# A four-stage transformer-like kernel on one Trainium2 core: slot table begun at half of its one-hots, gather started on source places alone, batch 2's shared products and the layer-2 gating moved

## The chip, the core and the metric

One Trainium2 (trn2) chip, one of its cores. The engines are TensorE (PE, with its weight loads as PEld), VectorE (DVE), ScalarE (ACT), GpSimd (POOL) and SyncE (SP). They run their own instruction streams and wait for one another through semaphores. The metric is the device time of one execution in microseconds; lower is better.

## The reference

Four stages on x of shape (4, 512, 128), each followed by a residual and a layer norm: attention, a mixture of experts (MoE) of 8 experts with one shared expert, a selective scan (state space), and a second, gated MoE with a shared expert. Each token goes to 2 of 8 experts. The two MoE layers are what this case is about; the second one, shortened:

```python
logits = x @ w_router
probs = jax.nn.softmax(logits, axis=-1)
top_w, top_i = jax.lax.top_k(probs, TOP_K)            # TOP_K = 2
mult = top_w / (top_w.sum(axis=-1, keepdims=True) + 1e-08)
w_full = zeros.at[jnp.arange(T)[:, None], top_i].set(mult)
for e in range(num_experts):                          # 8 experts, hidden 512
    h = jax.nn.silu(x @ w_gate[e]) * (x @ w_up[e])
    out = out + w_full[:, e:e + 1] * (h @ w_down[e])
hs = jax.nn.silu(x @ ws_gate) * (x @ ws_up)           # the shared expert
out = out + hs @ ws_down
```

The first MoE has one matrix with silu in place of the gated pair. In the whole, `x = _layernorm(x + stage(x))` four times.

## The kernel before, in words

T = 2048 tokens make 4 batches (b) of 512, or 16 tiles of 128. The layers run one after the other; `l` is 0 for the first MoE and 1 for the second (called layer 1 and layer 2 below). All engines' streams are written out by hand in this order of Python calls; nothing schedules them again.

An MoE layer does not compute all experts for all tokens. The 4096 (token, expert) pairs are sorted by expert into 39 slots of 128 rows (`ROUTED`), and each slot is multiplied with its one expert. To sort, `routing()` on DVE takes the top two experts of each token, PE counts (`counts()`), DVE makes places from the counts, then one-hot matrices: `slot_oh` and `marks` (L1393 to L1396) and the large one, `lane_oh`, 128 x 4096 (L1399). `table()` on PE (L596) multiplies the 32 pair groups' `lane_oh` with `marks`, 32 matmuls into PSUM bank 1; the sums hold for each slot row which token it gets. DVE meanwhile works out which expert each slot has (`past`, `slot_ef`, `slot_e`, L1402 to L1405, semaphore `expert_set`), then reads the table (L1411 to L1415: `source`, the token of each slot row; L1416 and L1417: `dest`, where the result row goes).

POOL then gathers the rows of the 39 slots from HBM with indirect DMAs (`rows<-xn_rows,source`, L1801), eight ahead into a ring, and scatters the slots' results (`y_choice`, L1807) by `dest`. Its first gather waits for `idx_set`, which the last of these DVE instructions raises.

The slot loop (`slot_steps`) is a software pipeline: PE turns the gathered rows of slot i+2 (L635 in layer 2, L663 in layer 1), DVE copies them to `xT` (L1441), PE multiplies slot i+1 (L641 and L645 in layer 2; L668 in layer 1), then slot i's down product. In layer 2 the gate and up weights of the slot's expert are first copied to fixed places: `own_g` by ACT, `own_u` by DVE (`own_weights`, L1434). After the loop, `combine` on DVE adds the two choices of each token, weighted with `gates`, which `gating()` (L1424 to L1430) has made.

The shared expert is done by batch: `shared_up`, then `shared_down` (L511, PSUM bank `2 + b % 2`), then `add_base` on DVE (L1479) adds x and frees the bank. `base_set` counts the `add_base`s. Batch 2 of layer 2 could reuse bank 2 only once batch 0's `add_base` had read it. In layer 2 the order on PE was `shared_down` of batches 0 and 1, the table, `shared_down` of batch 2; then PE waits for `base_set` to reach 3 before the slot loop. On DVE it was `lane_oh` (which waits for batch 1's `shared_down`, since it overlays that one's input), the slot experts, `add_base` 0 and 1, the table's reading, `add_base` 2, gating, `own_weights` of slots 0 and 1, the slot loop. In layer 1 the two `add_base`s and gating already stood behind the table's reading.

Of the kernel before, what the change touches and what calls it, by code (L numbers as in the profile page):

```python
# [20 lines left out]
ALU = mybir.AluOpType  # L21
# [4 lines left out]
P = 128  # L26
# [62 lines left out]
def build(nc, a, out):  # L89
    ctx = ExitStack()  # L90
    with ctx:
# [186 lines left out]
        onehot_set = layers("onehot_set", 1); table_ps = layers("table_ps", 1)  # L278
        expert_set = layers("expert_set", 1); idx_set = layers("idx_set", 1)
# [41 lines left out]
        x_bank, y_bank = ((0, 6), (0, 3)), ((1, 7), (1, 2))  # L321
        def slot_steps(step):

            for i in range(-2, ROUTED + 1):
                step(i)
# [110 lines left out]
        def _(pe):  # L436
# [68 lines left out]
            def shared_down(l, b, parts=range(QT)):  # L505
                pe.wait_ge(*sT_set[l].at((b + 1) * HB))
                if b >= 2:
                    pe.wait_ge(*base_set[l].at(b - 1))
                for q in parts:
                    for j in range(HB):  # L510
                        last = mm_(ps[:, 2 + b % 2, q * P:(q + 1) * P], (own_T[b] if l else sT[b % 2])[:, j, q * P:(q + 1) * P],  # L511
                                   (wd if l else w2)[:, NE * HID + j * D:NE * HID + (j + 1) * D], start=(j == 0), stop=(j == HB - 1))
                if QT - 1 in parts:
                    last.then_inc(sy_ps[l].sem, 1)
# [61 lines left out]
            def moe(l):  # L576
# [15 lines left out]
                def table():  # L592

                    pe.wait_ge(*onehot_set[l].at(1))
                    for g in range(PAIRS):
                        last = mm_(ps[:, 1, 0:2 * ROUTED], lane_oh[:, g, :], marks[:, g, :, :].rearrange("p c s -> p (c s)"),  # L596
                                   start=(g == 0), stop=(g == PAIRS - 1))
                    last.then_inc(table_ps[l].sem, 1)
# [6 lines left out]
                if l == 0:  # L605
                    shared_up(l, 1, (3,))
                    shared_down(l, 0)
                    shared_up(l, 2)
                    shared_down(l, 1)
                    table()  # L610
                    shared_up(l, 3)
                else:
                    shared_down(l, 0)
                    shared_down(l, 1)
                    table()
                    shared_down(l, 2)
# [622 lines left out]
        def _(dve):  # L1239
# [110 lines left out]
            def moe(l):  # L1350
# [8 lines left out]
                def routing():  # L1359
# [37 lines left out]
                    if l:  # L1397
                        dve.wait_ge(*sy_ps[1].at(2))
                    V.tensor_tensor(lane_oh, lane[:, :].unsqueeze(2).to_broadcast(by_lane),  # L1399
                                    count_up[:, :].unsqueeze(1).to_broadcast(by_lane), ALU.is_equal).then_inc(onehot_set[l].sem, 1)  # L1400
# [6 lines left out]
                    if l:  # L1407
                        add_base(l, 0)
                        add_base(l, 1)
# [5 lines left out]
                    link(V.tensor_scalar(source[:, :], held_i[:, :], T - 1, None, ALU.bitwise_and))  # L1415
# [35 lines left out]
                if l == 0:  # L1451
                    add_base(l, 0)
                    add_base(l, 1)
                else:
                    add_base(l, 2)
                gating()

                if l:
                    dve.wait_ge(*expert_set[1].at(1))
                    dve.wait_ge(*sT_set[1].at(3 * HB))  # L1460
                    own_weights(0)
                    own_weights(1)
                slot_steps(step)


                if l:
                    for b in range(NB):
# [8 lines left out]
            def add_base(l, b):  # L1476
                dve.wait_ge(*sy_ps[l].at(b + 1))
                dve.wait_ge(*(normed_set if l else kept)[l].at(b + 1))
                V.tensor_tensor(tiles(base[l][:, b * S:(b + 1) * S]), x_seq(b), tiles(bank(2 + b % 2)),  # L1479
# [199 lines left out]
        def _(pool):  # L1679
# [110 lines left out]
            def moe(l):  # L1790
# [6 lines left out]
                for i in range(ROUTED + RING):  # L1797
# [6 lines left out]
                    if i >= RING:  # L1804
                        y = i - RING
                        pool.wait_ge(*yout_set[l].at(y + 1))
# [57 lines left out]
```

## Time and profile before

| what | value |
|---|---|
| median of 3 runs | 665.77 us (664.08 to 669.92) |
| profiled execution | 664.27 us, its span 662.5 us |
| granted TensorE clock, mean | 0.95 |
| PE busy | 548.3 us (83%) |
| DVE busy | 420.4 us (63%) |
| POOL busy | 383.3 us (58%) |
| ACT busy | 361.1 us (55%) |

Layer 1's MoE lies at about 70 to 205 us of the span, the state space at 205 to 485, layer 2's MoE from 485 to the end. The granted clock is in shares of the full 2.4 GHz: 0.50 is 1.2 GHz. The profile gives for each instruction its start and length, the idle time of its engine before it in brackets, and what ended that idle time.

### The profile page before, as it was taken

What the parts mean: (1) busy time and instruction counts of PE and PEld (TensorE: products, weight loads), DVE (VectorE), ACT (ScalarE), POOL (GpSimd) and SP (SyncE); (2) the same over time, 40 slices, a digit from 0 to 9 for tenths busy, and PEclk for the clock granted to TensorE, in tenths of its full rate; (3) what the DMA queues carried; (4) which work ended last, traced back from release to release, by engine and by line L of the source; (5) the groups of instructions that cost most, each with busy time, mean ns of one, the idle gap of its engine ahead of it and who ended that gap; (6) DMA issues with size and microseconds to landing.
All of it is one profiled execution on the core that took longest, in us unless ns stands there. A gap on an engine that the chain in (4) does not pass through costs nothing.

```text
span 662.5 us, 8697 instructions
## 1 busy us (share of the span) xinstructions
PE 548.3 (83%) x2858; PEld 368.3 (56%) x2858; DVE 420.4 (63%) x754; ACT 361.1 (55%) x640; POOL 383.3 (58%) x303
## 2 busy tenths in 40 slices
PE   6988889999997559769967986989686899999980
PEld 3666556777665224225323532433246799999950
DVE  3444581111106899999999999999969444444446
ACT  3544564665552657944895597768332155555423
POOL 1011117777771246996697689678830677677451
PEclk9999998999999879889988998899998899999986
DMA  4154102111117754344334434433200111111142
GB/s 111 50 176 151 42 4 52 46 50 52 45 40 234 326 190 146 139 147 142 129 141 165 127 127 146 160 124 130 81 16 1 40 42 48 43 43 45 28 130 63
DMA packets 35147, 65.78 MB, mean 99 GB/s; under 512 B 6111, under 2 KB 23207, under 8 KB 34464
## 3 DMA queue, kind: packets, MB, share of 16 engines
q1 hardware_dynamic: 29824, 51.19, 22.9%
q0 software_dynamic: 4992, 9.32, 5.4%
q10 hardware_dynamic: 288, 4.72, 2.0%
q8 instruction: 24, 0.39, 0.2%
q14 instruction: 19, 0.16, 0.1%
HBM read 57.60 MB, written 8.52 MB: 100 GB/s over the span
## 4 chain that ended last, share of the span: by engine, by line
PE 39%; DVE 32%; issue 10%; POOL 8%; ACT 6%; DMA 5%; SPq 0%; DVEq 0%; POOLq 0%; ACTq 0%
DVE wide L1625 11%; DVE ps L1618 6%; PE ps L641 5%; PE ps L645 5%; DVE w L1625 5%; PE ps L653 5%; PE ps L668 4%; PE ps L681 4%; PE ps L792 3%; ACT work L1163 2%; PE ps L674 2%; DVE work L1490 2%; DVE work L1399 1%; POOL y_choice L1807 1%; POOL wide L1773 1%
## 5 line engine op out<-in xcount | busy, mean ns | idle before, releaser
L1801 POOL DMA_INDIRECT rows<-xn_rows,source x78 | 76.0, 974 | 61.5 <-DVE dest L1417 38.3
L1625 DVE TENSOR_TENSOR_SCAN wide<-work,ps 128x1024 f32<-128x1024 f32 x43 | 98.2, 2284 | 1.3
L792 PE MATMUL ps<-wide,ident 128*128 128x512 f32 x128 | 70.0, 675 | 26.7 <-POOL wide L1773 26.7
L1618 DVE TENSOR_TENSOR ps<-ps,w 128x1024 f32<-128x1024 f32 x64 | 78.9, 1233 | 7.1 <-DVE w L1625 0.5
L1441 DVE COPY xT<-ps 128x128 f32<-128x128 f32 x78 | 22.3, 287 | 81.7 <-PE ps L663 81.7
L1773 POOL TENSOR_TENSOR wide<-wide,w 128x1024 f32<-128x1024 f32 x22 | 51.8, 2356 | 32.9 <-DVE wide L1625 31.7
L792 PE MATMUL ps<-w,ident 128*128 128x512 f32 x124 | 61.4, 623 | 10.7 <-POOL w L1773 10.7
L1163 ACT ACTIVATE work<-work,a_neg 128x512 f32<-128x512 f32 x86 | 56.7, 711 | 19.8 <-DVE wide L1625 17.4
L1446 DVE TENSOR_TENSOR wide<-wide,ps 128x512 f32<-128x512 f32 x39 | 26.8, 687 | 61.9 <-PE ps L645 60.7
L792 PEld LDWEIGHTS ps<-wide,ident 128*128 128x128 f32 x128 | 24.1, 201 | 62.1 <-POOL wide L1773 39.9
L1773 POOL TENSOR_TENSOR w<-wide,w 128x1024 f32<-128x1024 f32 (+1 forms) x21 | 48.9, 2331 | 12.5 <-DVE wide L1625 12.2
L1807 POOL DMA_INDIRECT y_choice<-yout,dest x40 | 41.5, 1038 | 22.9 <-issue 11.4
L792 PEld LDWEIGHTS ps<-w,ident 128*128 128x128 f32 x124 | 24.8, 205 | 46.8 <-issue 25.3
L1807 POOL DMA_INDIRECT y_choice<-pre,dest x38 | 39.7, 1046 | 19.1 <-issue 9.4
L1625 DVE TENSOR_TENSOR_SCAN w<-rows,ps 128x1024 f32<-128x1024 f32 x21 | 48.0, 2284 | 0.6
L641 PE MATMUL ps<-xT,wide 128*128 128x128 f32 x312 | 42.1, 279 | 2.3 <-DVE xT L1441 2.3
L668 PE MATMUL ps<-w,xT 128*128 x78 | 41.9, 620 | 0.9 <-DVE xT L1441 0.9
L1026 ACT ACTIVATE wide<-ps 128x512 f32<-128x512 f32 x39 | 23.3, 597 | 35.4 <-PE ps L668 35.4
L645 PE MATMUL ps<-xT,wide 128*128 128x128 f32 x312 | 42.1, 279 | 0.0
L653 PE MATMUL ps<-wd,wide 128*128 x312 | 41.3, 275 | 0.0
L681 PE MATMUL ps<-w,wide 128*128 x312 | 41.2, 275 | 0.0
L641 PEld LDWEIGHTS ps<-xT,wide 128*128 128x128 f32 x312 | 38.7, 195 | 2.5 <-DVE xT L1441 2.5
(273 smaller groups left out, 1172.9 us busy)
## 6 DMA issues: line engine op xcount, KB each, us to landing
w<-bc_rows SPq DMA_DIRECT2D x64, 512.0 KB, 3.7
w<-in_w ACTq DMA_DIRECT2D x2, 2304.0 KB, 9.1
w<-y_choice SPq DMA_DIRECT2D x16, 256.0 KB, 3.8
wg<-in_wg SPq DMA_DIRECT2D x1, 2304.0 KB, 12.1
wu<-in_wu SPq DMA_DIRECT2D x1, 2304.0 KB, 17.0
wd<-in_wd SPq DMA_DIRECT2D x1, 2304.0 KB, 22.0
rows<-xn_rows,source POOLq DMA_INDIRECT x78, 2.5
work<-in_x SPq DMA_DIRECT2D x4, 256.0 KB, 2.9
```

What stands on the lines that cost most here:

```text
L641: last = mm_(ps[:, hbank[0] + p, j * P:(j + 1) * P], own_g[p][:, j * P:(j + 1) * P], xT[p][:, :], start=True, stop=True)
L645: last = mm_(ps[:, hbank[1] + p, j * P:(j + 1) * P], own_u[p][:, j * P:(j + 1) * P], xT[p][:, :], start=True, stop=True)
L653: last = mm_(bank(y_bank[1][p], D), hs[p][:, j * P:(j + 1) * P], wc[:, ds(e + j * D, D)], start=(j == 0), stop=(j == HB - 1))
L668: last = mm_(bank(hbank[0] + p), xT[p][:, :], wa[:, ds(e, HID)], start=True, stop=True)
L681: last = mm_(bank(y_bank[l][p], D), hT[p][:, j * P:(j + 1) * P], wc[:, ds(e + j * D, D)], start=(j == 0), stop=(j == HB - 1))
L792: last = mm_(bank(6 + h), ident[:, :], hc[j % 4][:, h, :], start=False, stop=(j == NS - 1))
L1163: last = A(dA[n % 3][:, h, lo:S], delta[n // NS % 2][:, h, lo:S], ACT.Exp, scale=a_neg[:, j + h * NS:j + h * NS + 1])
L1618: V.tensor_tensor(dbu, du, bc_all[j % 4][:, 0:S].unsqueeze(1).to_broadcast([P, EH, S]), ALU.mult)\
L1625: V.tensor_tensor_scan(st[n % 3].rearrange("p h t -> p (h t)"), dA[n % 3].rearrange("p h t -> p (h t)"), dbu.rearrange("p h t -> p (h t)") ...
L1773: G.tensor_tensor(hc[j % 4][:, 0:own, :], st[n % 3][:, 0:own, :], bc_all[j % 4][:, S:2 * S].unsqueeze(1).to_broadcast([P, own, S]), ALU.mu ...
L1801: G.indirect_dma_start(out=xin[i % RING][:, :], out_offset=None, in_=xn_rows, in_offset=bass.IndirectOffsetOnAxis(ap=source[:, i:i + 1], a ...
L1807: G.indirect_dma_start(out=y_choice, out_offset=bass.IndirectOffsetOnAxis(ap=dest[:, y:y + 1], axis=0), in_=yout[y % RING][:, :], in_offse ...
```

## The change

Five edits:

1. `lane_oh` is made in two DVE instructions of 128 x 2048 in place of one of 128 x 4096, each raising `onehot_set`. `table()` waits for the first ahead of matmul 0 and for the second ahead of matmul 16. Both layers.
2. `idx_set` is raised twice: by the instruction that makes `source`, and by the one that makes `dest`. The gather waits for the first; the first scatter waits for the second. Both layers.
3. Layer 2, PE: `shared_down` of batch 2 stands ahead of the table. It writes bank 7 (`sy_bank`) in place of bank 2, and no longer waits for batch 0's `add_base`.
4. Layer 2, DVE: `add_base` 0 and 1 stand behind the table's reading, with `add_base` 2.
5. Layer 2, DVE: `gating()` stands behind the slot loop, ahead of `combine`.

The diff, cut to these:

```diff
-        onehot_set = layers("onehot_set", 1); table_ps = layers("table_ps", 1)
-        expert_set = layers("expert_set", 1); idx_set = layers("idx_set", 1)
+        onehot_set = layers("onehot_set", 2); table_ps = layers("table_ps", 1)
+        expert_set = layers("expert_set", 1); idx_set = layers("idx_set", 2)
...
+        def sy_bank(l, b):
+
+            return 7 if l and b == 2 else 2 + b % 2
...
             def shared_down(l, b, parts=range(QT)):
                 pe.wait_ge(*sT_set[l].at((b + 1) * HB))
-                if b >= 2:
+                if b >= 2 and not (l and b == 2):
                     pe.wait_ge(*base_set[l].at(b - 1))
                 for q in parts:
                     for j in range(HB):
-                        last = mm_(ps[:, 2 + b % 2, q * P:(q + 1) * P], (own_T[b] if l else sT[b % 2])[:, j, q * P:(q + 1) * P],
+                        last = mm_(ps[:, sy_bank(l, b), q * P:(q + 1) * P], (own_T[b] if l else sT[b % 2])[:, j, q * P:(q + 1) * P],
...
                 def table():
 
-                    pe.wait_ge(*onehot_set[l].at(1))
                     for g in range(PAIRS):
+                        if g % (PAIRS // 2) == 0:
+                            pe.wait_ge(*onehot_set[l].at(g // (PAIRS // 2) + 1))
...
                     shared_down(l, 0)
                     shared_down(l, 1)
+                    shared_down(l, 2)
                     table()
-                    shared_down(l, 2)
...
-                    V.tensor_tensor(lane_oh, lane[:, :].unsqueeze(2).to_broadcast(by_lane),
-                                    count_up[:, :].unsqueeze(1).to_broadcast(by_lane), ALU.is_equal).then_inc(onehot_set[l].sem, 1)
+                    by_half = [P, PAIRS // 2, P]
+                    for i in range(2):
+                        own = slice(i * PAIRS // 2, (i + 1) * PAIRS // 2)
+                        V.tensor_tensor(lane_oh[:, own, :], lane[:, own].unsqueeze(2).to_broadcast(by_half),
+                                        count_up[:, :].unsqueeze(1).to_broadcast(by_half), ALU.is_equal).then_inc(onehot_set[l].sem, 1)
...
-                    if l:
-                        add_base(l, 0)
-                        add_base(l, 1)
                     dve.wait_ge(*table_ps[l].at(1))
...
-                    link(V.tensor_scalar(source[:, :], held_i[:, :], T - 1, None, ALU.bitwise_and))
+                    V.tensor_scalar(source[:, :], held_i[:, :], T - 1, None, ALU.bitwise_and).then_inc(idx_set[l].sem, 1)
...
                 else:
-                    add_base(l, 2)
-                gating()
-
-                if l:
                     dve.wait_ge(*expert_set[1].at(1))
                     dve.wait_ge(*sT_set[1].at(3 * HB))
+                    for b in range(3):
+                        add_base(l, b)
                     own_weights(0)
                     own_weights(1)
+                if l == 0:
+                    gating()
                 slot_steps(step)
 
                 if l:
+                    gating()
                     for b in range(NB):
...
+                        if y == 0:
+                            pool.wait_ge(*idx_set[l].at(2))
                         pool.wait_ge(*yout_set[l].at(y + 1))
```

What this does to the order of the instructions, at three places of layer 2. First PE, from the counts to the first slot: L589 and L590 are the counts, L511 `shared_down`, L596 the table, L635 the turned rows of slots 0 and 1, L641 slot 0's gate product. Before:

```order
L589 MATMUL ps<-mask,before 128x128
L590 MATMUL ps<-mask,ones 128x128
L511 MATMUL ps<-wd,work 128x128 x32
L596 MATMUL ps<-work 128x78 x32
L511 MATMUL ps<-wd,work 128x128 x16
L635 MATMUL ps<-ident,rows 128x128 x2
L641 MATMUL ps<-xT0,wide 128x128 x4
```

And now (the lines have moved by 4 and 5):

```order
L593 MATMUL ps<-mask,before 128x128
L594 MATMUL ps<-mask,ones 128x128
L515 MATMUL ps<-wd,work 128x128 x48
L601 MATMUL ps<-work 128x78 x32
L640 MATMUL ps<-ident,rows 128x128 x2
L646 MATMUL ps<-xT0,wide 128x128 x4
```

The 16 products of batch 2 have moved from behind the table to ahead of it. Second DVE, from `lane_oh` to the first reading of the table. Before:

```order
L1399 TENSOR_TENSOR work<-lane,count_up 128x4096
L1402 TENSOR_TENSOR work<-slot_row,ends 128x312
L1404 TENSOR_REDUCE slot_ef<-work 128x39
L1405 TENSOR_SCALAR slot_e<-slot_ef 128x39
L1479 TENSOR_TENSOR work<-x_all,ps 128x512 x2
L1411 COPY vacant<-ps 128x39
```

And now:

```order
L1407 TENSOR_TENSOR work<-lane,count_up 128x2048 x2
L1410 TENSOR_TENSOR work<-slot_row,ends 128x312
L1412 TENSOR_REDUCE slot_ef<-work 128x39
L1413 TENSOR_SCALAR slot_e<-slot_ef 128x39
L1416 COPY vacant<-ps 128x39
```

The one-hots are in two pieces, and the two `add_base`s (L1479) are gone from ahead of the reading. Third DVE, from `dest` to the first weight copies. Before:

```order
L1417 SCALAR_TENSOR_TENSOR dest<-held,vacant 128x39
L1479 TENSOR_TENSOR work<-x_all,ps 128x512
L1424 TENSOR_REDUCE zsum<-sc 128x16
L1425 TENSOR_SCALAR zsum<-zsum 128x16
L1426 TENSOR_TENSOR den<-zsum,egap 128x16
L1429 RECIPROCAL gates0<-den 128x16
L1430 TENSOR_TENSOR gates1<-gates0,egap 128x16
L350 TENSOR_LOAD slot_e
L1434 ISA
L1434 COPY wide<-wu 128x512
L1434 ISA
L1434 COPY wide<-wu 128x512
```

And now:

```order
L1422 SCALAR_TENSOR_TENSOR dest<-held,vacant 128x39
L1485 TENSOR_TENSOR work<-x_all,ps 128x512 x3
L354 TENSOR_LOAD slot_e
L1439 ISA
L1439 COPY wide<-wu 128x512
L1439 ISA
L1439 COPY wide<-wu 128x512
```

Behind `dest` there are now three `add_base`s and no gating. In layer 1 only the one-hots are in two pieces; its DVE and PE order is otherwise the same.

## Rows read from the trace of the kernel before

**Rows 1.** Chain that ended last, 485 to 530 us: start, length (us), engine, tile, line

```profile
505.72 4.34 DVE work L1399
510.11 2.26 PE ps L596 x32
512.37 4.67 PE ps L511 x32
520.73 1.67 PE ps L641 x8
```

**Rows 2.** Timeline, layer 1, table: start, length, engine, line, tiles, [idle before <-releaser]

```profile
88.36 4.42 DVE L1399 TENSOR_TENSOR work<-lane,count_up 128x4096 bf16<-128x4096 bf16 x1
...
92.83 1.35 PE L596 MATMUL ps<-work 128*128 128x78 bf16 x32 [1.05 <-DVE work L1399]
...
93.71 0.18 DVE L1405 TENSOR_SCALAR slot_e<-slot_ef 128x39 int32<-128x39 f32 x1
...
94.22 0.20 DVE L1411 COPY vacant<-ps 128x39 f32<-128x39 f32 x1 [0.33 <-PE ps L596]
...
95.45 0.20 DVE L1417 SCALAR_TENSOR_TENSOR dest<-held,vacant 128x39 uint32<-128x39 f32 x1
```

**Rows 3.** Timeline, layer 1, gathers and scatters on POOL, slot 1's turn on PE

```profile
96.59 1.23 POOL L1801 DMA_INDIRECT rows<-xn_rows,source  x1 [22.88 <-DVE dest L1417]
...
98.13 0.94 POOL L1801 DMA_INDIRECT rows<-xn_rows,source  x1 [0.30 <-issue]
...
100.70 0.33 PE L663 MATMUL ps<-ident,rows 128*128 128x128 f32 x1 [0.88 <-DMA rows<-xn_rows,source]
...
109.02 1.03 POOL L1807 DMA_INDIRECT y_choice<-yout,dest  x1 [1.22 <-ACT yout L912]
...
195.64 0.98 POOL L1807 DMA_INDIRECT y_choice<-pre,dest  x1 [1.17 <-ACT pre L912]
```

**Rows 4.** Timeline, layer 2, from shared_down to dest

```profile
496.49 7.31 PE L511 MATMUL ps<-wd,work 128*128 128x128 f32 x64
...
511.09 1.28 DVE L1479 TENSOR_TENSOR work<-x_all,ps 128x512 f32<-128x512 f32 x2
...
512.41 0.20 DVE L1411 COPY vacant<-ps 128x39 f32<-128x39 f32 x1
...
513.20 0.18 DVE L1415 TENSOR_SCALAR source<-held_i 128x39 uint32<-128x39 uint32 x1
...
513.64 0.20 DVE L1417 SCALAR_TENSOR_TENSOR dest<-held,vacant 128x39 uint32<-128x39 f32 x1
```

**Rows 5.** Timeline, layer 2, from the first gather to the first xT copies

```profile
514.12 1.11 POOL L1801 DMA_INDIRECT rows<-xn_rows,source  x1 [15.45 <-DVE dest L1417]
515.54 0.95 POOL L1801 DMA_INDIRECT rows<-xn_rows,source  x1 [0.30 <-issue]
...
517.07 0.69 DVE L1479 TENSOR_TENSOR work<-x_all,ps 128x512 f32<-128x512 f32 x1 [3.23 <-PE ps L511]
...
519.64 0.84 DVE L1434 COPY wide<-wu 128x512 f32 x2 [0.77 <-DVE gates L1430]
520.40 0.47 DVE L1441 COPY xT<-ps 128x128 f32<-128x128 f32 x2
```

**Rows 6.** Busy by stretch, layer 2: length; PE, PEld, DVE, ACT, POOL (instructions); clock, DMA, GB/s

```profile
510.10:512.20 2.10, 2.09 (x33) 2.09 (x33) 2.03 (x5) 0.37 (x1) 0.00 (x0) 0.50 0.00 0
512.20:517.10 4.90, 4.83 (x35) 4.64 (x32) 1.45 (x9) 0.78 (x2) 2.36 (x3) 0.78 0.06 13
...
520.70:524.10 3.40, 3.37 (x17) 3.37 (x18) 0.17 (x1) 1.11 (x2) 2.67 (x3) 0.57 0.29 60
524.10:527.00 2.90, 2.90 (x26) 2.90 (x25) 2.04 (x4) 0.60 (x1) 0.95 (x1) 0.91 0.20 51
```

**Rows 7.** The slot loop of layer 2 by stretch, columns as in rows 6

```profile
528.30:614.80 86.50, 86.50 (x778) 86.50 (x777) 38.10 (x93) 43.55 (x94) 63.32 (x61) 1.00 0.17 43
```

**Rows 8.** Timeline, layer 2, DVE's first combine

```profile
638.98 3.32 DVE L1490 SCALAR_TENSOR_TENSOR work<-w,gates,work 128x128 f32<-128x128 f32 x8 [8.79 <-DMA w<-y_choice]
```

More of the change, by code:

```diff
@@ L1478, in add_base @@
                 dve.wait_ge(*(normed_set if l else kept)[l].at(b + 1))
-                V.tensor_tensor(tiles(base[l][:, b * S:(b + 1) * S]), x_seq(b), tiles(bank(2 + b % 2)),
+                V.tensor_tensor(tiles(base[l][:, b * S:(b + 1) * S]), x_seq(b), tiles(bank(sy_bank(l, b))),
                                 ALU.add).then_inc(base_set[l].sem, 1)
```

## The prediction

> **What bounds the kernel now.** I read the chain that ended last first, for the two places that the change touches, then the timelines there, then the busy shares by stretch to see who paces what follows. The reader is to see three things.
>
> In layer 2 the chain from the routing to the first slot is DVE's `lane_oh` (505.72 to 510.06), PE's table (to 512.37), PE's `shared_down` of batch 2 (to 517.04), and, after DVE's `add_base` 2, gating and weight copies, slot 0's first product at 520.73 [rows 1, 5]. Of these only the table is needed for the slots' rows. PE finished batches 0 and 1 at 496.49 + 7.31 = 503.80 [rows 4] and then stood idle until 510.11, because the table waited for the one-hots.
>
> From there on the slot loop belongs to PE: in 528.30 to 614.80 it is busy 86.50 of 86.50 us at a granted clock of 1.00 [rows 7]. A slot has 25 PE records (1 turn and three times 8), so 778 records are 31.1 slots of 2.78 us. Nothing in the loop has slack for PE, and nothing else holds it, so the loop's end moves with its start.
>
> In layer 1 POOL paces. From its first scatter at 109.02 it goes on with 0.30 us between instructions until one waits for ACT at 195.64 [rows 3]; 31 gathers and 36 scatters of about 1.0 us with those gaps fill that time. So here too an earlier first gather, and with it an earlier first scatter, moves the layer's end.
>
> **The change, layer 1.** The one-hots ended at 88.36 + 4.42 = 92.78, the table ran 92.83 to 94.18, and DVE, done with the slot experts at 93.71 + 0.18 = 93.89, waited 0.33 us for it [rows 2]. Two halves cost the fixed part of one more DVE instruction: not under nothing, not over 0.18 us, which is what a whole 128x39 instruction takes [rows 4]. Neighbours that don't depend on each other overlap a little, so I take 0.1. PE does the first 16 matmuls during the second half, and the last 16 take half of 1.35, 0.68, from 92.93 to 93.6. That is ahead of DVE's slot experts (93.99 with the 0.1), so DVE goes on without a wait at about 93.95 instead of 94.22, 0.27 earlier. `source` is done 0.97 us after that start (in layer 2, 512.41 to 513.38 [rows 4]), at 94.92. The gather waited for `dest`, done at 95.65 [rows 2]. The release comes 0.73 earlier. The gather started 0.94 after its release (96.59 [rows 3]), against 0.28 in layer 2 (513.84 to 514.12 [rows 4, 5]); no row says what the other 0.66 is. If it goes with the release it stays, and the gain is 0.73; if it was a fixed moment that the first gather had to wait for, the gain is between 0.07 and 0.73; if it vanishes, 1.39. I take **0.7**, since the rows show nothing that POOL waits for but `dest`. The table's earlier end also starts `shared_up` of batch 3 about 0.6 earlier, which keeps ACT's last silu out of the way. The scatter's new wait for `dest` is met 13 us before the first scatter and costs nothing; even if the cover were gone it would be 0.46, the distance from `source` to `dest`.
>
> **Layer 2, the table.** Batch 2's 32 matmul records now run from 503.80 and take half of 7.31, 3.66, at the full clock at which the 64 before them ran: to 507.5. They need no bank wait, and their input was ready (PE never stopped for it before). The first half of the one-hots is there at 505.72 + 2.2 = 507.95, so they are hidden with 0.45 us to spare. The second half is there at 510.16; its 16 matmuls take 0.68 at full clock and 1.13 at the lower one (half of 2.26 [rows 1], a stretch at 0.50 [rows 6]); PE has just worked, so I take 0.7 and the table is done at 510.9. DVE's slot experts end at 511.2 (the `add_base` behind them started at 511.09 [rows 4], plus 0.1). So DVE reads the table at **511.2, not 512.41**: the table and the two `add_base`s that ended together at 512.37 are both off the path. `source` is done at 512.17, the first gather starts 0.28 later at 512.45 instead of 514.12 [rows 5], 1.67 earlier.
>
> **Layer 2, the first slot.** Two chains meet. DVE: `dest` at 512.63, three `add_base`s of 1.28 + 0.69 = 1.97 [rows 4, 5], so 514.60; then the 0.77 us of reading `slot_e` into registers that stood ahead of the weight copies [rows 5], so these start at 515.37; `xT` follows 0.76 after (519.64 to 520.40 [rows 5]), at 516.13, and the first one is done at about 516.4. Gathers: the second one starts 1.42 after the first, at 513.87; in layer 1 PE turned the same slot 2.57 after that gather's start (98.13 to 100.70 [rows 3]), so 516.44. PE does slot 1's turn ahead of slot 0's product, so that begins about 0.25 later, at **516.7 instead of 520.73, 4.0 earlier**. The two chains are within 0.3 us, so one of them being off doesn't cost much, one of them being late costs all that it is late.
>
> What I cost at nothing: gating, 1.1 us (five small instructions between the end of `add_base` 2 at 517.76 and the register load at 519.64 - 0.77 = 518.87 [rows 5]), now behind the loop, where DVE waited 8.79 us for the scattered rows [rows 8]; without that cover 1.1 us. The three `add_base`s ahead of the weight copies hold back PE too (it waits for `base_set` at 3), but that is 514.60, ahead of the first turn. ACT's `own_g` copies wait for `slot_e`, 0.1 later than before and with some 4 us in hand.
>
> **The clock.** It was 0.50 in the table's stretch after 6.3 us of idle PE, 0.78 in the next one, 0.57 at the first slot and 0.91 after it [rows 6]. In full-clock time the first slots lost 3.40 x 0.43 + 2.90 x 0.09 = 1.72 us. With the change PE is idle from 510.9 to 516.7 but for two turns, 5.8 us where it was 3.7, so the start may look like the table's: 2.10 x 0.50 + 4.90 x 0.22 = 2.13 lost. The difference, **0.4**, is a cost of the change; it is between nothing (the same loss as before) and the rival below. The Trainium skill, "TensorE: Matmul & The Clock Gate", Part 1, says the idle state of the array is the throttled one and activity releases it, and that idle gaps cost a new warm-up; rows 6 show the 0.50 after the idle stretch and the return during work. By that page's rule the longer idle ahead of the loop speaks against the change, and what the rule would make of it at worst is the third rival.
>
> **Sum.** 0.7 + 4.0 - 0.4 = 4.3 us. Against the profiled execution's own 664.27: 660.0. The median of the runs is 665.77, 1.5 above it, with 664.08 the lowest, so the same sum against the median is 661.5. I take 660.8, between.
>
> **Rivals.**
> - *A late landing or a stall at the first slots takes back 1 to 2 us* (20%). For it: everything up to the first slot is a chain of small links, each of which showed spread (0.28 and 0.94 from release to first gather [rows 3 to 5]); a second gather that lands 1 us late moves slot 0 by 1 us, and so does a slower register load. Against: nothing in rows 5 stalled. Gain 2.3 to 3.3: 661 to 662 on the profile's time, up to 663.5 on the median's.
> - *More than the sum* (10%): layer 1's 0.66 vanishes and the clock costs nothing more, 0.66 + 0.4 on top: gain 5.4, 658.9 to 660.4.
> - *Slower: the clock stays low into the loop* (5%). The idle stretch ahead of the loop is longer, and the first slots have waits on silu and on DVE between products, so PE might not come back after two slots. Each slot done at half clock costs 2.78 us more [rows 7]. The gain of 4.3 is gone after 1.5 such slots beyond those of before, and 1% is lost after 4 (4 x 2.78 = 11.1, so 671 on the profile's time). Against: in rows 6 the clock came back to 0.91 within the second slot though its waits were the same.
> - *The change does not reach the loop* (5%): if slot 0 were held by something that doesn't move, as ACT's weight copies, only the 0.7 of layer 1 and what of the gather's 1.67 counts would stay: 662 to 663.6.
>
> **How the numbers follow.** The forecast itself, a gain of 3.3 to 5.2, has 60%: 659.1 to 662.5 between both bases. The range leaves out the clock's bad case and the far end of each of the others: 657.5 to 664.5. About 1% (6.7 us) is what a measurement of this kernel can tell from no change; the runs of before lie 5.8 apart. A gain over 6.7 needs the second rival and a low draw: 8%. A loss over 6.7 needs four slots at half clock: 3%. Within 1%: 89%.
>
> **What would show it.** Right: the table's second half 16 matmuls right behind the second half one-hots, DVE going on from `slot_e` to reading the table without idle in both layers; the first gather of layer 2 about 1.7 us earlier in distance from `lane_oh`'s start (6.7 instead of 8.4), slot 0's product at 11.0 from it instead of 15.0; gating right behind the loop with DVE still idle ahead of `combine`; slots of 2.79 us. Wrong: a clock of 0.50 over more than the first two slots; idle time of PE ahead of slot 0 longer than to 11 us from `lane_oh`'s start, and then what releases it (the gather, DVE's `xT`, ACT); in layer 1 a first gather less than 0.5 us earlier, or POOL idle between scatters.

## Result and the profile after

| | before | after |
|---|---|---|
| median of 20 runs each on one chip | 669.49 us (663.89 to 671.97) | 664.65 us (660.34 to 667.02) |
| ratio, 95% interval | | 0.9937 (0.9918 to 0.9956) |
| profiled execution: time, span | 664.27, 662.5 us | 663.71, 661.9 us |
| mean granted clock | 0.95 | 0.94 |
| PE, DVE, POOL, ACT busy | 548.3, 420.4, 383.3, 361.1 us | 554.6, 419.7, 383.4, 361.4 us |

The change gains 0.63% of 669.49, 4.2 us (4.8 by the two medians), where 4.3 was forecast. That is inside the 1% which the prediction took as no change, though the interval of 20 and 20 executions leaves out 1. The time itself, 664.65, lies 0.15 above the range, because the forecast started from too low a base. The 20 times of before fall into two groups with nothing between 665.8 and 668.4: five from 663.89 to 665.77 and fifteen from 668.49 to 671.97. The profile shown of before (664.27) is of the lower group, and so are two of the three runs shown. Those of after: two at 660.34 and 660.87, eighteen from 663.50 to 667.02, the profiled one (663.71) among these. Lower group against lower group (medians) it is 664.65 to 660.6, upper against upper 669.70 to 664.8. So the two profiles differ by 0.56 us only, while the kernels differ by 4.2.

The timeline of after in layer 2, from the one-hots to the first slots, in the columns of [rows 2]. The one-hots begin at 508.40, against 505.64 before (in the DVE timeline; the chain of [rows 1] has 505.72); distances below are from that start.

```profile
508.40 4.48 DVE L1407 TENSOR_TENSOR work<-lane,count_up 128x2048 bf16<-128x2048 bf16 x2
...
510.74 0.76 PE L601 MATMUL ps<-work 128*128 128x78 bf16 x16 [0.60 <-DVE work L1407]
512.94 0.76 PE L601 MATMUL ps<-work 128*128 128x78 bf16 x16 [1.44 <-DVE work L1407]
513.92 0.19 DVE L1416 COPY vacant<-ps 128x39 f32<-128x39 f32 x1
515.17 1.11 POOL L1807 DMA_INDIRECT rows<-xn_rows,source  x1 [13.73 <-DVE source L1420]
515.19 1.88 DVE L1485 TENSOR_TENSOR work<-x_all,ps 128x512 f32<-128x512 f32 x3
516.99 0.80 DVE L1439 COPY wide<-wu 128x512 f32 x2
517.98 0.45 PE L640 MATMUL ps<-ident,rows 128*128 128x128 f32 x1 [4.27 <-DMA rows<-xn_rows,source]
519.15 0.48 PE L640 MATMUL ps<-ident,rows 128*128 128x128 f32 x1 [0.73 <-DMA rows<-xn_rows,source]
519.42 1.92 PE L646 MATMUL ps<-xT,wide 128*128 128x128 f32 x8
521.13 1.91 PE L650 MATMUL ps<-xT,wide 128*128 128x128 f32 x8
```

It is what the change was to do: half of the table's matmuls run during the second half of the one-hots, the other half (0.76 us) behind it, the gather is released by `source`, three `add_base`s stand behind `dest`, and slot 0's product starts at 519.42 - 508.40 = 11.02 from the one-hots' start, where before had 520.73 - 505.64 = 15.09. Slot 0's two groups of eight products take 1.92 and 1.91 us, at half clock. The chain of waits of after for the same place (start, length, what):

```profile
508.48 4.40 DVE work L1407 x2
512.88 0.41 DVE work L1410
...
513.32 0.49 DVE slot_ef L1412
...
514.70 0.20 DVE source L1420
514.90 0.28 issue
515.17 1.11 POOL rows L1807
516.28 0.30 issue
516.59 2.52 DMA rows<-xn_rows,source
519.11 0.04 issue
519.15 0.48 PE ps L640
```

Against [rows 1], PE's table and `shared_down` are gone from it; DVE's slot experts and the landing of the second gather stand in their place.

### The profile page after: what moved, and what is told of

The parts are those of the page before. It is cut to its first block, busy times and chain, and to the rows that moved or that the text cites. A ratio compares the mean times of both kernels' runs of the same rounds, so it can differ in the third digit from the quotient of the medians.

```text
span 661.9 us, 8700 instructions
## 1 busy us (share of the span) xinstructions
PE 554.6 (84%) x2858; PEld 370.4 (56%) x2858; DVE 419.7 (63%) x756; ACT 361.4 (55%) x640; POOL 383.4 (58%) x303
## 4 chain that ended last, share of the span: by engine, by line
PE 36%; DVE 34%; issue 10%; POOL 9%; ACT 6%; DMA 3%; SPq 0%; POOLq 0%; DVEq 0%; ACTq 0%
DVE wide L1631 11%; DVE ps L1624 6%; PE ps L646 5%; PE ps L650 5%; DVE w L1631 5%; PE ps L658 5%; PE ps L673 4%; PE ps L797 3%; PE ps L686 3%; ACT work L1168 2%; PE ps L679 2%; POOL rows L1807 2%; DVE work L1496 2%; POOL y_choice L1815 1%; DVE work L1407 1%
## 5 line engine op out<-in xcount | busy, mean ns | idle before, releaser
L797 PE MATMUL ps<-wide,ident 128*128 128x512 f32 x128 | 72.1, 691 | 24.6 <-POOL wide L1779 24.6
L797 PE MATMUL ps<-w,ident 128*128 128x512 f32 x124 | 63.5, 641 | 10.5 <-POOL w L1779 10.5
```

What stands on the lines that cost most here:

```text
L797: last = mm_(bank(6 + h), ident[:, :], hc[j % 4][:, h, :], start=False, stop=(j == NS - 1))
```

## What holds the last norm: where the two groups come from

The traces differ ahead of the part that was changed. Before layer 2's one-hots, PE waits 1.94 us for the last layer norm in both kernels. The PE timeline of before:

```profile
490.64 0.66 PE L809 MATMUL ps<-ident,x_all 128*128 128x128 f32 x4 [1.94 <-ACT x_all L1139]
...
491.64 1.03 PE L819 MATMUL ps<-gate,nT_all 128*128 128x8 f32 x8 [0.35 <-ACT nT_all L912]
...
492.53 1.10 PE L501 MATMUL ps<-nT_all,wg 128*128 128x512 f32 x2
```

and of after:

```profile
490.41 1.00 PE L814 MATMUL ps<-ident,x_all 128*128 128x128 f32 x4 [1.94 <-ACT x_all L1144]
...
491.55 1.84 PE L824 MATMUL ps<-gate,nT_all 128*128 128x8 f32 x8
493.24 2.06 PE L505 MATMUL ps<-nT_all,wg 128*128 128x512 f32 x2
```

The same instructions behind the same wait take 0.66, 1.03 and 1.10 us in the one and 1.00, 1.84 and 2.06 in the other. The busy shares by stretch (columns as in [rows 6]) give the clock, first of before:

```profile
490.40:494.00 3.60, 3.01 (x16) 2.09 (x17) 1.12 (x6) 0.85 (x3) 0.79 (x1) 1.00 0.24 73
```

then of after:

```profile
490.50:494.00 3.50, 3.36 (x13) 2.71 (x14) 0.51 (x3) 0.77 (x2) 0.47 (x1) 0.51 0.25 75
494.00:497.00 3.00, 3.00 (x5) 1.22 (x4) 2.25 (x13) 0.00 (x0) 0.00 (x0) 0.50 0.00 0
```

It was 1.00 before and about 0.50 (1.2 of 2.4 GHz) after, from the wait until 497. From ACT's last piece of the norm (489.71 before, 489.48 after) to the one-hots that is 505.64 - 489.71 = 15.93 us against 508.40 - 489.48 = 18.92, 3.0 us. I take this distance, **norm to one-hots**, from every run below. (The expectations of after again and w_before count it from DVE's part of the norm, 1.0 to 1.3 us earlier.)

So the 0.56 us between the two profiles can be added up: 0.23 earlier at the last norm, 2.99 later from there to the one-hots, 3.28 earlier from these to slot 0's result: 0.52. With the clock at the norm taken out, the two profiles differ by 0.56 + 2.99 = 3.55 us.

## Experiments

The runs came from four chips. On that of m1 to m4 (one edit taken back each) before took 669.08 us; on the other three 703 to 705. Ratios are always against before on the same chip. "First result" is ACT's first copy of a slot's result (`yout`).

**Before again, and PE kept busy at the two waits.** The first experiments fill PE's waits with products of 128x512 that nobody reads. `fill(2)` stands ahead of the last norm in w_last, `fill(4)` ahead of layer 2's slots in w_slots; w_all has both, and one such product ahead of layer 1's slots.

```diff
+            def fill(n):
+                for _ in range(n):
+                    mm_(bank(0), ident[:, :], nT_all[:, 0:S], start=True, stop=True)
...
             shared_up(1, 2, (0, 1))
+            pe.wait_ge(*nT_set[1].at(NB - 1))
+            fill(2)
             turn_last()
...
-                pe.wait_ge(*expert_set[l].at(1))
                 pe.wait_ge(*counts_taken[l].at(1))
+                if l:
+                    fill(4)
+                pe.wait_ge(*expert_set[l].at(1))
                 pe.wait_ge(*base_set[l].at(2 + l))
```

> The kernel before, unchanged, profiled once more. Theory 'clock lottery': its times lie in two groups (about 664 to 666 and 668.5 to 672), and they differ in whether TensorE's granted clock falls in PE's wait for the last layer norm, ahead of layer 2's last router products. In a run of the slow group the stretch of 485 to 500 us shows 0.50 during those products (none in the profile shown) and the one-hots of layer 2 start 3 us or more later than at 505.6; in a run of the fast group both are as in the profile shown. Rival 'memory': the slow group's extra time lies in the state space or in the weight loads (205 to 485 us), and the stretch 485 to 500 is the same in both.

> The changed kernel with two more 128x512 products, whose result nobody reads, in PE's wait for the last layer norm (layer 2, ahead of the last turn). They take 1.7 of about 2.1 us that PE is idle. Clock lottery: the granted clock stays 1.00 from 485 to 500 us in every profile, and the median comes down by 2 to 3 us against the changed kernel (ratio to before 0.989 to 0.991 in place of 0.9937), with few runs left in the slow group. Rival: the slow group has its time elsewhere, the median stays within 1 us of the changed kernel's (ratio about 0.9937).

> The changed kernel with four such products (3.4 us) in PE's wait between the table and the first gathered rows of layer 2. If the 0.50 at the first slots is a cost of the idle stretch, the clock stays 1.00, and the distance from the one-hots' start to the loop's steady beat shrinks by 1.7 to 2.3 us; slot 0's product still starts 11.0 us after the one-hots' start. Rival: the first slots are held by the chain of silu, product and weight copies and not by the clock, and the distance shrinks by less than 0.5.

> The changed kernel with both fillings and one such product in layer 1 between shared_up of batch 3 and the first gathered rows. If the clock costs add up, 4 to 6 us below the changed kernel's median: ratio to before 0.984 to 0.988. In layer 1 one product fills 0.86 of 3.5 us, so there the 0.50 may stay. Rival: no more than w_last or w_slots alone.

Measured, before 703.92: before again 0.9994 (0.9972 to 1.0016), w_last 0.9897 (0.9867 to 0.9927), w_slots 0.9945 (0.9920 to 0.9971), w_all 0.9893 (0.9858 to 0.9927). The timeline of w_last (its first row counts the filling too):

```profile
511.29 1.88 PE L453 MATMUL ps<-nT_all,ident 128*128 128x512 f32 x4
...
513.38 0.66 PE L819 MATMUL ps<-ident,x_all 128*128 128x128 f32 x4 [0.22 <-ACT x_all L1151]
...
514.39 1.03 PE L829 MATMUL ps<-gate,nT_all 128*128 128x8 f32 x8 [0.35 <-ACT nT_all L924]
```

The wait is 0.22 instead of 1.94, the products behind it take 0.66 and 1.03 as in the lower group's profile, norm to one-hots is 15.92. Before again, with the unfilled wait, had 19.06. w_all was forecast at 0.984 to 0.988 if the clock's costs added up; it came out at that of w_last, so its rival held. The filling ahead of the slots did its work there and no more. The timeline of w_slots:

```profile
538.40 1.07 PE L653 MATMUL ps<-xT,wide 128*128 128x128 f32 x8
...
543.10 1.06 PE L653 MATMUL ps<-xT,wide 128*128 128x128 f32 x8
...
545.63 0.61 PE L657 MATMUL ps<-xT,wide 128*128 128x128 f32 x4 [0.92 <-issue]
548.03 2.07 PE L665 MATMUL ps<-wd,wide 128*128 x8 [1.78 <-DVE wide L1458]
```

Slot 0's product runs at full clock (1.07), and slot 2's begins 543.10 - 527.55 = 15.55 from the one-hots' start, 2.7 ahead of after (526.63 - 508.40 = 18.23). Yet behind slot 2's start PE stands 0.92 us waiting on issue and 1.78 us for DVE, its next products take 2.07 us, half clock again, and the first result comes 19.67 us from the one-hots' start, where after again has 19.66. The time, 0.9945, is that of the change without the filling (0.9941 below). In the seven profiled executions of after again, w_last, w_slots, w_all, c_w_last, c_w_all and m5, all on these three chips, the first result lies at 19.62 to 19.76, though slot 0's product starts at 10.85 to 11.63: on them it is not slot 0's product that sets it. What does was not found. The slot loop has such stalls throughout there (last section); a chip of the 665 us kind wasn't tried with it, so whether the first slots' clock is worth anything there stays open.

**One edit taken back at a time**, the other four kept. The edits by the numbers of the change: m1 makes the one-hots in one instruction (1), m2 lets the gather wait for `dest` (2),

```diff
-                pool.wait_ge(*idx_set[l].at(1))
+                pool.wait_ge(*idx_set[l].at(2))
```

m3 puts batch 2's `shared_down` behind the table, still in bank 7 (3), and m4 the `add_base`s 0 and 1 ahead of its reading (4):

```diff
-                    shared_down(l, 2)
                     table()
+                    shared_down(l, 2)
...
+                    if l:
+                        add_base(l, 0)
+                        add_base(l, 1)
                     dve.wait_ge(*table_ps[l].at(1))
```

> The changed kernel with edit 1 taken back (one DVE instruction of 128x4096 for the one-hots). All numbers in us from the start of layer 2's one-hots; the changed kernel has table read at 5.52, gather at 6.77, slot 0's product at 11.02. By the prediction's steps the table starts at 4.5 and takes 1.35 at full clock, so DVE waits for it until 5.87: gather at 7.1, product at 11.35; with the clock at half, table read at 6.8, gather 8.0, product 12.3. If the halves bring nothing (DVE's slot experts are the end anyway) nothing moves.

> The changed kernel with edit 2 taken back (the gather waits for dest as before). Us from the start of layer 2's one-hots: gather at 7.1 in place of 6.77, product at 11.35 in place of 11.02, because slot 0's product follows the second gather's landing; in layer 1 the gather 0.3 later (7.75 in place of 7.43). Rival: DVE's three add_bases and weight copies are what slot 0 waits for, and the product stays at 11.0.

> The changed kernel with edit 3 taken back in its order (batch 2's shared_down behind the table, still in bank 7). Us from the start of layer 2's one-hots: gather unchanged at 6.77; shared_down ends at 9.0 at full clock or up to 10.3 at half, add_base 2, the weight copies and xT behind it, slot 0's product at 11.5 to 12.8. Rival: the gathers are the later chain anyway and the product stays at 11.0.

> The changed kernel with edit 4 taken back (add_base of batches 0 and 1 ahead of the reading of the table). Us from the start of layer 2's one-hots: table read at 6.8 in place of 5.52, gather at 8.05, slot 0's product at 12.3 in place of 11.02, as the second gather's landing decides. If the DVE chain decided, the product would stay, since DVE's sum is the same.

| distance from the one-hots' start, layer 2, us | before | after | m1 | m2 | m3 | m4 |
|---|---|---|---|---|---|---|
| table read by DVE | 6.77 | 5.52 | 5.86 | 5.53 | 5.80 | 6.71 |
| first gather | 8.48 | 6.77 | 7.12 | 7.10 | 7.06 | 7.97 |
| slot 0's product | 15.09 | 11.02 | 11.38 | 11.31 | 13.67 | 12.29 |
| first result | 21.60 | 18.32 | 18.65 | 18.47 | 18.55 | 19.13 |
| fifth result | 32.75 | 29.48 | 29.81 | 29.62 | 29.70 | 30.29 |
| ratio to before | 1 | 0.9937 | 0.9916 | 0.9958 | 0.9945 | 0.9978 |
| its 95% interval | | .9918-.9956 | .9879-.9953 | .9919-.9997 | .9918-.9973 | .9949-1.0007 |

m1, m2 and m4 came out within 0.1 us of what was expected of the distances. The times can't tell m1, m2 and m3 from the whole change, nor from each other; m4, the edit that is worth most alone, lies highest, though its interval overlaps theirs. Taken back singly, the four cost 0.33, 0.14, 0.22 and 0.81 us at the fifth result, 1.5 together of the 3.27 that all five bring (the fifth was taken back on another chip): each opens only as far as the others let it.

m3 was a miss. Its gather was expected unchanged at 6.77 and came at 7.06, since the table's halves took 1.22 us each, half clock, in place of 0.76. Slot 0's product was expected between 11.5 and 12.8 and came at 13.67. Its timeline:

```profile
517.63 6.12 PE L515 MATMUL ps<-wd,work 128*128 128x128 f32 x32
...
525.74 1.16 PE L646 MATMUL ps<-xT,wide 128*128 128x128 f32 x8 [0.65 <-DVE xT L1446]
526.73 1.06 PE L650 MATMUL ps<-xT,wide 128*128 128x128 f32 x8
```

PE had stood 4.17 us ahead of the table and 0.98 within it; the granted clock is 0.50 over the table and 0.61 over the 32 products behind it, which take 6.12 us in place of 3.6. So `add_base` 2 and all behind it are late. But PE then meets the slots at full clock (1.16, 1.06 against 1.92, 1.91), and the first result is 0.23 later only. The order of after pays for its earlier start with a slow clock in the slots; the other order runs the same slow stretch off before them.

**The change again, gating taken back, and before with the filling**, on a chip where before took 703.23. m5 has `gating()` back behind the three `add_base`s (5); w_before is the kernel before with `fill(2)` ahead of the last norm.

> The changed kernel once more, against the kernel before on the same chip. If the change is worth its 4.3 us whatever the clock does at the last norm, the ratio is 0.992 to 0.995 again. From the start of layer 2's one-hots: gather 6.77, slot 0's product 11.0 again; from the last norm's application to the one-hots either 16.9 or 20.2, the two states of the clock.

> The changed kernel with edit 5 taken back (gating between the add_bases and the weight copies). Us from the start of layer 2's one-hots: DVE ends the add_bases at 8.7, gating at 9.8, the copies at 10.6 (11.4 if the 0.77 of register load comes back), xT at 10.9 to 11.7. The second gather's row is turned by 11.0. So slot 0's product moves by 0 to 0.7 in place of the whole 1.1. By the recorded prediction, whose two chains were within 0.3, it moves by about 0.8.

> The kernel before with the two unread products in PE's wait for the last norm, and nothing else. Clock lottery: the distance from the last norm's application to the one-hots is 16.9 to 17.2 in place of 20.3, and the median is 2.5 to 3.3 us under the kernel before's (ratio 0.995 to 0.996). It has none of the five edits, so what it gains is the clock's alone. Rival: no difference.

After again 0.9941 (0.9918 to 0.9965): the same gain on the other kind of chip. m5 0.9960 (0.9934 to 0.9987): slot 0's product at 11.63, 0.6 later than in after again, within the 0 to 0.7 expected. From the timeline of m5:

```profile
537.41 0.76 DVE L1439 COPY wide<-wu 128x512 f32 x2 [0.77 <-DVE gates L1435]
...
538.43 2.07 PE L646 MATMUL ps<-xT,wide 128*128 128x128 f32 x8 [0.40 <-DVE xT L1446]
```

Now PE waits for DVE. But the first result stands at 19.65 against 19.66 in after again, so on this chip nothing of the 0.6 was left there; edit 5 alone is not shown to be worth anything. w_before 0.9962 (0.9943 to 0.9981), 2.7 us of 703.23, with none of the five edits; norm to one-hots 15.92. m5, without filling, had 15.92 too and was profiled at 697.03, the lowest of its ten.

**The filling once more, and useful work in its place**, before 704.92. In u_useful the table stands ahead of batch 2's `shared_down` and `add_base` 2 behind the weight copies, so that PE works right up to the slots without reading dummies; u_both adds the last norm's `fill(2)`.

```diff
-                    shared_down(l, 2)
                     table()
+                    shared_down(l, 2)
...
-                    for b in range(3):
-                        add_base(l, b)
+                    add_base(l, 0)
+                    add_base(l, 1)
                     own_weights(0)
                     own_weights(1)
+                    add_base(l, 2)
```

> The changed kernel with two unread products in PE's wait for the last norm, again, beside three others on one chip. Ratio to the kernel before 0.989 to 0.991: the change's 4.3 us and the 3 us of the clock in three executions of four.

> The changed kernel with unread products in all three waits (two at the last norm, four between layer 2's table and its gathered rows, one in layer 1). Where no engine stalls on instruction issue in the slot loop, the 2.3 us that the filling of the second wait brings from the one-hots to slot 1's product reach the end: first result copied 16.0 us after the one-hots' start in place of 18.3, and the ratio is 0.986 to 0.988. If the loop takes it back, the ratio is that of the run with the last norm's filling alone.

> The changed kernel with batch 2's shared_down behind the table again, as useful work in the wait for the gathers, and DVE's order add_base 0 and 1, weight copies, add_base 2. Us from the start of layer 2's one-hots: shared_down ends at 9.0 to 11.7 by the clock that it finds, slot 0's product at 11.0 to 13.2 but at full clock, first result copied at 16.2 to 18.0 in place of 18.32. Ratio 0.991 to 0.994. Rival: it ends like the run with edit 3 alone taken back, first result at 18.55 and no gain.

> The kernel of u_useful with two unread products in PE's wait for the last norm. 3 us under u_useful in three executions of four: ratio 0.987 to 0.990.

Measured: c_w_last 0.9921 (0.9890 to 0.9952), c_w_all 0.9920 (0.9893 to 0.9948), u_useful 0.9979 (0.9954 to 1.0003), u_both 0.9933 (0.9910 to 0.9956). c_w_all has its first result at 19.76, where 16.0 was expected if the loop did not take it back: its other case held, the ratio is that of c_w_last. u_useful was expected at 0.991 to 0.994, with the first result at 16.2 to 18.0. It failed for m3's reason, as its timeline shows:

```profile
535.63 5.87 PE L515 MATMUL ps<-wd,work 128*128 128x128 f32 x32
...
543.12 1.16 PE L646 MATMUL ps<-xT,wide 128*128 128x128 f32 x8 [0.28 <-DVE xT L1446]
```

The products run at half clock for most of their 5.87 us (granted 0.63); slot 0's begin at 13.05 and the first result comes at 20.54, 0.9 behind after again. u_both, with its median 3.1 us under that of u_useful, gains it back at the last norm, but misses its 0.987 to 0.990. The changed kernel with `fill(2)` at the last norm has 0.9897 and 0.9921 of before (0.9893 and 0.9920 with the other fillings too), the changed kernel alone 0.9937 and 0.9941. So it is the best version by its point values. It was never timed beside the changed kernel on one chip, and its intervals overlap that one's (0.9918 to 0.9956), so how much better it is than the change alone is not shown; the filling's own worth is measured on the kernel before (w_before).

Over all profiled executions, norm to one-hots was 15.92 or 15.93 us in six of six with that filling, and without it 15.92 or 15.93 in two of eleven (before and m5) and 18.92 to 19.29 in nine (before again, after, after again, m1 to m4, w_slots, u_useful). In six of these nine the four turns right behind the wait still took 0.65 or 0.66 us, full clock, and only the products behind them 1.44 to 1.85. So the same program comes out of this one wait either way (before 15.93, before again 19.06, on different chips), and PE's idle time decides it, since filling it removes the slow case. That it is drawn anew in each execution is inferred from the times of one chip, which fall into groups.

The mean granted clock, which every execution has, goes with the groups on the chips of 665 to 670 us. Of after's 20 it is 0.950 in the two lowest and at most 0.949 in the others. Of the 27 executions of before on the chip of m1 to m4, the nine from 663.84 to 667.01 have 0.950, the eighteen from 667.61 to 673.10 have 0.938 to 0.948. On that chip the gap between the groups is not empty, though (666.04, 667.01, 667.61), and one execution of m4 has 0.950 at 666.56. That the last norm makes the whole of the groups is not shown: they lie 4 to 5 us apart, the distance explains 3.0 to 3.4. And executions differ ahead of it too: on these chips the last norm (ACT's last piece) is reached at 489.71 (before), 489.48 (after), 493.94, 488.46, 492.78 and 489.70 (m1 to m4), and m1 and m3, the latest, were the longest of their eight executions. What moved them was not looked into.

## Why the prediction was right or wrong

**The base: the failed step.** "I take 660.8, between" took the profile's 664.27 and the median of three, 665.77. Both are of the lower group, one execution in four of this kernel; the sum of 4.3 from 669.49 gives 665.2, 0.5 from the measured 664.65. The sign was in front of me: one of the three runs, 669.92, stood 5.8 above the lowest, and I named that spread only as a bound on what can be measured, where it should have widened the range upward. What the runs show in its place is a base of 669.49, with fifteen of twenty executions at 668.49 or above; 3.0 of the 5 us between the groups go with the clock at the last norm, and the rest stays open. The changed kernel's own lower group lies at 660.6, near the 660.0 predicted from the lower group's profile, but it is two runs in twenty.

**Layer 1: 0.7, measured 0.77 to 0.80.** Timeline of after, layer 1:

```profile
93.01 0.76 PE L601 MATMUL ps<-work 128*128 128x78 bf16 x16 [0.54 <-DVE work L1407]
...
93.98 0.19 DVE L1416 COPY vacant<-ps 128x39 f32<-128x39 f32 x1
...
95.07 0.20 DVE L1422 SCALAR_TENSOR_TENSOR dest<-held,vacant 128x39 uint32<-128x39 f32 x1
95.89 1.23 POOL L1807 DMA_INDIRECT rows<-xn_rows,source  x1 [22.08 <-DVE dest L1422]
```

DVE reads the table at 93.98 without a wait (forecast 93.95), `source` ends at 94.94 and the gather starts 0.95 later: the 0.94 of [rows 3] went with its release, as taken; what it is stays unknown. The row puts the gather's wait down to `dest`, which ended at 95.27, though the code waits for `source` alone, and m2 shows the difference: with the wait for `dest` it starts 0.32 later. From the one-hots' start the gather moved from 8.23 to 7.43 and the first scatter from 20.66 to 19.89. Of that 0.77, 0.54 was left at the scatter that waits for ACT (195.64 [rows 3], now 195.10), since these one-hots began 0.10 later and the loop took 0.13 longer; 0.46 at layer 1's `combine` and 0.23 at the last norm. These last steps are the difference of one execution of each and may be noise: m1 to m4 reach the last norm up to 5.5 us apart. The prediction let all of layer 1's 0.7 reach the end; no run shows that it did.

**Slot 0's product: 4.0, measured 4.07.** Forecast 11.0 from the one-hots' start, measured 11.02. The gather chain gave it, link by link: table read at 5.52 (forecast 5.5), gather at 6.77 (6.7), the turn of slot 1 at 10.75 (10.7). The DVE chain, which I put within 0.3 us of it, was 1.1 faster than forecast: the weight copies started at 516.99, 8.6 us from the one-hots' start where the sum has 9.7, before the last `add_base` had ended in the record, and the 0.77 us of reading `slot_e` ahead of them [rows 5] did not appear. In m5, with gating there again, it did. So the read follows gating's last small instruction at a price and the `add_base`s at none; why, no run here shows.

**The clock: 0.4, measured 0.8, the one term that was mis-sized.** From slot 0's product to the first result it took 21.60 - 15.09 = 6.51 us before and 18.32 - 11.02 = 7.30 after. Busy by stretch of after:

```profile
516.40:520.40 4.00, 1.69 (x7) 1.43 (x8) 1.97 (x6) 0.00 (x0) 2.90 (x4) 0.50 0.20 49
520.40:524.40 4.00, 4.00 (x21) 4.00 (x20) 1.22 (x3) 1.11 (x2) 3.08 (x4) 0.50 0.28 51
524.40:528.40 4.00, 4.00 (x36) 4.00 (x36) 1.23 (x3) 1.99 (x4) 2.12 (x3) 0.96 0.22 53
```

The start did not look like the table's stretch, as assumed. PE ran at 0.50 from slot 0's product at 519.42 to 524.7: about 5.3 x 0.50 = 2.65 us lost where before had lost 1.72 and I had put 2.13. It had been idle for 4.27 us ahead of the first turn. m3 and w_slots are the counterproof: with work there, slot 0's two products run at full clock (1.16 and 1.06 us in the one, 1.07 and 1.06 in the other). The gain at the first result is therefore 4.07 - 0.79 = 3.28 and not 3.6, and with layer 1's 0.77, if all of it reached the end, the sum is 4.05. The two profiles, with the clock at the norm taken out, have 3.55, which is 3.28 and the 0.23 of layer 1 that was left. Measured are 4.2 by the ratio (2.9 to 5.5 by its interval), and 4.05 and 4.9 from group to group. So the mechanism was right, but that 4.3 meets 4.2 this closely is in part luck: the interval would have held 3.5 as well. The Trainium skill, "TensorE: Matmul & The Clock Gate", Part 1, says that one and the same kernel has more or fewer slow matmuls from run to run, by the phase at its start, and that the ramp costs less than 1% of a typical kernel. The traces agree in size (3.0 us of 664), but show the draw at a wait in the middle of the kernel, and it was larger than all errors of the sum together.

**The loop and gating.** The loop's row of after, against [rows 7]:

```profile
528.90:615.20 86.30, 86.30 (x776) 86.30 (x775) 37.95 (x94) 43.55 (x93) 63.01 (x61) 1.00 0.17 45
```

PE is busy throughout again, so its start sets its end: the last gate product stands at 626.93, from 627.45. Gating lies behind the loop and is hidden, as the DVE timeline shows:

```profile
629.59 0.28 DVE L1429 TENSOR_REDUCE zsum<-sc 128x16 f32<-128x128 f32 x1
...
638.37 3.33 DVE L1496 SCALAR_TENSOR_TENSOR work<-w,gates,work 128x128 f32<-128x128 f32 x8 [7.58 <-DMA w<-y_choice]
```

DVE's wait for the rows fell from 8.79 [rows 8] to 7.58, the 1.2 us of gating.

**The rivals.** A late landing (20%) did not come: each link named above was on time. More than the sum (10%): neither of its conditions held. The slow clock into the loop (5%) did not come: it was back at 524.7, within slot 1. The change not reaching the loop (5%): it reached it whole. What decided the number had no rival: that the kernel before itself takes 669.7 in three executions of four. Such a rival leaves the gain alone and puts the time at 669.7 - 4.3 = 665.4.

## What to carry to other kernels

Before adding up a change of under 1%, find out which of the kernel's own times the profile belongs to: if a few runs lie 1% apart, forecast for each group, and look in the trace for a PE wait of some 2 us behind which the same instructions have taken half or full clock. What edits that open one chain together bring is not the sum of what each costs when taken back: 1.5 of 3.3 us here, for four of the five. Moving PE's work ahead of a wait starts the next stage earlier but colder; a few unread products in a short wait can be worth more (2.7 us at the last norm, by w_before) than the reordering of useful ones (0.2 for edit 3 at the first result), or nothing (w_slots, on a chip whose slot loop stalls).

## What the hardware showed beside this

Three of the chips ran the kernel before at 703 to 705 us instead of 669. The costliest groups of before, from the page of the kernel before on the first chip (count, busy us, mean ns, idle before):

```profile
L668 PE MATMUL ps<-w,xT 128*128 x78 | 41.9, 620 | 0.9 <-DVE xT L1441 0.9
```

and of before again, on a chip of the other kind:

```profile
L668 PE MATMUL ps<-w,xT 128*128 x78 | 44.8, 659 | 10.3 <-issue 6.3
L681 PE MATMUL ps<-w,wide 128*128 x312 | 44.1, 288 | 3.0 <-issue 3.0
```

Layer 1's slot loop by stretch, before and before again:

```profile
109.02:195.64 86.62, 84.19 (x547) 64.58 (x545) 9.89 (x34) 49.49 (x109) 65.63 (x66) 1.00 0.18 48
```

```profile
110.28:216.00 105.72, 91.32 (x532) 66.90 (x531) 9.45 (x33) 48.12 (x108) 65.76 (x66) 0.94 0.14 39
```

The engines do the same work with the same busy time (POOL 65.63 and 65.76), but the loop takes 105.72 us in place of 86.62: of the 14.4 us that PE stands there, the profile puts 10.8 down to nothing but issue, while ACT waits mostly for PE and POOL, beside its 0.30 us between instructions, for ACT. The cause wasn't looked into. The ratio of the change was the same on both kinds, 0.9937 and 0.9941, though the distances inside the loop were not.
